# Layer-1 edge pass of a graph network: state sums interleaved with the next block, semaphores for drains, powers in PSUM

## What is computed

```python
# N, E, NIN, H, C = (6250, 100000, 256, 8, 32); per edge, then summed by target node dst
e     = edge_attr @ We                         # E x 256
k, v  = k[src] + e, v[src] + e
logit = (q[dst] * k).sum(channels)             # E x 8
alpha = softmax of logit over the edges of one dst
out   = segment_sum(v * alpha, dst)
```

## Time and profile before

| | |
|---|---|
| time, median of 3 runs | 5678.94 us (5672.48 to 5680.9) |
| span of the profiled execution | 5673.3 us |
| busy in the span | TensorE 50%, VectorE 67%, ScalarE 25%, GpSimd 60% |
| the edge pass | about 3504 to 5156 us of the span |
| in it, per 100 us | VectorE 90.2, TensorE 82.2, GpSimd 77.1, ScalarE 24.1 us busy; DMA engines 1.01 of the time |

### The profile page before, as it was taken

The page is one execution under the profiler, slowest core; times in us unless marked ns, Lnnn a source line. Parts: engine busy times, 40 slices in busy tenths (PEclk is TensorE's granted clock), DMA queues, the critical chain, the costliest instruction groups (busy, mean ns, idle before and its releaser), DMA issues. The chain is left out here.

```text
span 5673.3 us, 49658 instructions
## 1 busy us (share of the span) xinstructions
PE 2860.0 (50%) x13052; PEld 2232.1 (39%) x13052; DVE 3824.3 (67%) x6117; ACT 1441.9 (25%) x2526; POOL 3388.4 (60%) x3382
## 2 busy tenths in 40 slices
PE   7513200000000000015899986888888888884777
PEld 5412200000000000014677633777776777673456
DVE  7357778786454545546543464989899998995763
ACT  1113333332233333311222211222222222221320
POOL 0267777777777777753440276777777777773200
PEclk9655555555555555556799998999999999896888
DMA  3133344432363333323232355999999999993114
GB/s 101 36 84 108 107 130 148 130 104 83 103 220 110 109 110 109 110 87 124 93 124 68 107 191 191 317 319 323 319 319 321 319 323 318 323 318 113 67 47 148
DMA packets 290231, 961.79 MB, mean 170 GB/s; under 512 B 79248, under 2 KB 119831, under 8 KB 248468
## 3 DMA queue, kind: packets, MB, share of 16 engines
q0 software_dynamic: 171296, 483.60, 28.6%
q1 hardware_dynamic: 118788, 476.59, 24.9%
HBM read 626.03 MB, written 345.69 MB: 171 GB/s over the span
## 5 line engine op out<-in xcount | busy, mean ns | idle before, releaser
L1249 PE MATMUL e_psE<-e_we,e_eaT 128*128 128x256 f32 x3136 | 903.5, 415 | 279.3 <-DVE e_wv L1148 179.3
L1111 POOL DMA_INDIRECT e_kv<-kv,rec x784 | 875.7, 1117 | 266.3 <-issue 253.7
L779 POOL DMA_INDIRECT g_g<-t,rec x784 | 777.1, 991 | 254.0 <-issue 253.7
L779 POOL DMA_INDIRECT g_g<-t,dst_of x784 | 743.6, 949 | 259.3 <-issue 257.2
L1249 PEld LDWEIGHTS e_psE<-e_we,e_eaT 128*128 128x128 f32 x3136 | 649.4, 210 | 400.7 <-ACT e_eaT L1192 299.4
L1407 PE MATMUL j_psM<-ident,tail 128*128 128x128 f32 x32 | 7.2, 416 | 1149.0 <-PEq L53 1149.0
L1250 PE MATMUL e_psE<-e_kv,ident 128*128 128x256 f32 x1568 | 509.8, 409 | 0.0
L816 DVE TENSOR_TENSOR_SCAN g_wv<-g_fx,g_wv 128x2176 f32<-128x2176 f32 x98 | 459.0, 4684 | 0.2 <-issue 0.2
L1407 PEld LDWEIGHTS j_psM<-ident,tail 128*128 128x128 f32 x32 | 6.8, 322 | 1149.8 <-issue 1149.8
L1118 POOL DMA_INDIRECT e_q<-q,q_of x392 | 370.9, 946 | 119.7 <-issue 119.7
L956 ACT ACTIVATE g_st<-g_wv 128x2048 f32<-128x2048 f32 x98 | 375.9, 3836 | 0.0
(11 more groups left out here) (519 smaller groups left out, 6620.8 us busy)
## 6 DMA issues: line engine op xcount, KB each, us to landing
state<-e_st SPq DMA_DIRECT2D x98, 1088.0 KB, 6.2
e_ea<-in_edge_attr SPq DMA_DIRECT2D x98, 896.0 KB, 9.8
state_f<-g_st SPq DMA_DIRECT2D x49, 1088.0 KB, 4.4
state_b<-g_st SPq DMA_DIRECT2D x49, 1088.0 KB, 4.3
m_work<-xs SPq DMA_DIRECT2D x119, 128.0 KB, 2.3
ys<-m_work SPq DMA_DIRECT2D x119, 128.0 KB, 1.7
xs<-g_ta SPq DMA_DIRECT2D x28, 512.0 KB
g_g<-t,rec POOLq DMA_INDIRECT x784
```

What stands on the lines that cost most here:

```text
L779: pool.indirect_dma_start(g[:, u, j, :], None, tab, bass.IndirectOffsetOnAxis(ap=at_, axis=0)).then_inc(gat[u], 16)
L1111: pool.indirect_dma_start(kv[:, u, b, :], None, c.kv, bass.IndirectOffsetOnAxis(ap=c.rec[:, t, 1:2], axis=0)).then_inc(gkv[u][b // 4], 16)
L1249: nc.tensor.matmul(half, eaT[:, m, j, k, :], we[:, k, :], start=(k == 0), stop=False)
```

## The change

It concerns `edge_pass` alone; the arithmetic stays the same.

- VectorE: the chain of L1176 of a block (`chain`) and its denominators' scan (`denominators`) are issued between the instructions of the next block, one `step` at a time. Drains are replaced by semaphores that VectorE raises and waits for itself (`chained`, `weighed`, `multiplied`, `logits`, `scanned`, `carried`, `entered`). The reduction is split in two halves; the second addition of values moves behind `ex`. `wv` gets two buffers.
- ScalarE makes the exponential twice: into `cw` as before, and for the products into `pw`, which lies in a PSUM bank. Maximum and denominator of a block are stored after the next block's start.
- TensorE has three transpose banks instead of four (the fourth is `pw`), `eaT` has two buffers, and block n+1 is transposed between the two halves of block n.
- GpSimd gathers the first four keys and values, then the queries, then the other four, with a wait before each.
- SyncE loads the attributes three blocks ahead instead of two.

The diff; the removed lines of VectorE, ScalarE and TensorE stand above in the kernel, and are left out here.

```diff
--- before.py
+++ after.py
@@ -1037,22 +1037,24 @@
...
-        eaT = sb("eaT", [P, 4, 2, 2, P])
+        eaT = sb("eaT", [P, U, 4, 2, 2, P])
...
-        psT = [pb(f"psT{n}") for n in range(4)]
+        psT = [pb(f"psT{n}") for n in range(3)]
...
+        pw = pb("pw")[:, 0:H * B].rearrange("p (h b) -> p h b", h=H)
...
-        wv, before = sb("wv", [P, B, D]), sb("before", [P, D])
+        wv, before = sb("wv", [P, U, B, D]), sb("before", [P, D])
...
-        ld, gq0, gq1, eg0, eg1, used, exd, cwd, dnd, std, so0, so1, free, dump, tp, tcp, ep, ed = (
-            sem(n) for n in ("ld", "gq0", "gq1", "eg0", "eg1", "used", "exd", "cwd", "dnd", "std", "so0",
+        ld, gq0, gq1, eg0, eg1, exd, cwd, dnd, std, so0, so1, free, dump, tp, tcp, ep, ed = (
+            sem(n) for n in ("ld", "gq0", "gq1", "eg0", "eg1", "exd", "cwd", "dnd", "std", "so0",
...
-        q_used = sem("q_used")
...
+        chained, weighed, multiplied, logits, scanned, carried, entered = (sem(n) for n in (
+            "chained", "weighed", "multiplied", "logits", "scanned", "carried", "entered"))
...
@@ -1077,50 +1079,68 @@
...
-            def store(i, u):
-                blk = i * U + u
+            def store(blk, u, older):
...
-                sp.wait_ge(so[1 - u], (i + 1) * 16)
+                sp.wait_ge(so[1 - u], older * 16)
...
+            def ahead(blk, u, older):
+                sp.wait_ge(tp, blk * 4 + 8)
+                c.alone(sp)
+                load_attributes(blk + 3, 1 - u)
+                store(blk, u, older)
...
-            with sp.Fori(0, NBLK // U - 1) as i:
-                for u in range(U):
-                    sp.wait_ge(tp, (i * U + u + 1) * 4)
-                    c.alone(sp)
-                    load_attributes(i * U + u + U, u)
-                    store(i, u)
-            store(NBLK // U - 1, 0)
-            store(NBLK // U - 1, 1)
+            sp.wait_ge(tp, 4)
+            c.alone(sp)
+            load_attributes(2, 0)
+            ahead(0, 0, 1)
+            with sp.Fori(0, NBLK // U - 2) as i:
+                ahead(i * U + 1, 1, i + 1)
+                ahead(i * U + 2, 0, i + 2)
+            store(NBLK - 3, 1, NBLK // U - 1)
+            store(NBLK - 2, 0, NBLK // U)
+            store(NBLK - 1, 1, NBLK // U)
...
+            def keys_and_values(blk, half):
+                for b in range(4 * half, 4 * half + 4):
+                    t = blk * B + b
+                    pool.indirect_dma_start(kv[:, blk % U, b, :], None, c.kv, bass.IndirectOffsetOnAxis(
+                        ap=c.rec[:, t, 1:2], axis=0)).then_inc(gkv[blk % U][half], 16)
...
-                u = blk % U
...
-                    pool.wait_ge(used, blk - U + 1)
+                    pool.wait_ge(ed, 4 * (blk - U) + 6)
...
-                for b in range(B):
-                    t = blk * B + b
-                    pool.indirect_dma_start(kv[:, u, b, :], None, c.kv, bass.IndirectOffsetOnAxis(
-                        ap=c.rec[:, t, 1:2], axis=0)).then_inc(gkv[u][b // 4], 16)
+                keys_and_values(blk, 0)
...
-                    pool.wait_ge(q_used, blk - U + 1)
+                    pool.wait_ge(logits, 3 * (blk - U + 1))
...
-                    pool.indirect_dma_start(q[:, u, m, :], None, pairs, bass.IndirectOffsetOnAxis(
-                        ap=c.q_of[:, t // 2:t // 2 + 1], axis=0)).then_inc(gq[u], 16)
+                    pool.indirect_dma_start(q[:, blk % U, m, :], None, pairs, bass.IndirectOffsetOnAxis(
+                        ap=c.q_of[:, t // 2:t // 2 + 1], axis=0)).then_inc(gq[blk % U], 16)
+                if blk >= U:
+                    pool.wait_ge(ed, 4 * (blk - U) + 8)
+                    c.alone(pool)
+                keys_and_values(blk, 1)
...
+            flat = lambda a: a.rearrange("p h b -> p (h b)")
+            back = lambda a: a.rearrange("p h b -> p (h b)")[:, ::-1]
...
@@ -1132,64 +1152,121 @@
...
+            def chain(n, u, b):
+                if b == 0:
+                    v.wait_ge(free, n + 1)
+                    v.wait_ge(weighed, n + 1)
+                else:
+                    v.wait_ge(chained, n * (B - 1) + b)
+                nc.vector.scalar_tensor_tensor(
+                    out=st[:, u, b, 0:D], in0=st[:, u, b - 1, 0:D] if b else before[:], scalar=kept[:, u, b:b + 1],
+                    in1=wv[:, u, b, :], op0=ALU.mult, op1=ALU.add).then_inc(std if b == B - 1 else chained, 1)
+            def denominators(n, u):
+                v.wait_ge(entered, n + 1)
+                v.wait_ge(act_mt, n)
+                nc.vector.tensor_tensor_scan(flat(den[:]), flat(kept_h[:, u]), flat(cw[:]), 0.0, ALU.mult,
+                                             ALU.add).then_inc(dnd, 1)
+            def one_block(n, u, gathered, later):
+                def step(b):
+                    if later:
+                        chain(n - 1, 1 - u, b)
+                def half_of(half):
+                    quad = psE[:, half * 1024:(half + 1) * 1024]
+                    return quad, q[:, u, 2 * half:2 * half + 2, :].rearrange("p m n -> p (m n)")
+                def with_queries(half):
+                    quad, q4 = half_of(half)
+                    v.wait_ge(ep, n * 4 + 2 * half + 2)
+                    tt(q4, quad, q4, ALU.mult).then_inc(multiplied, 1)
+                def values(half):
+                    quad, _ = half_of(half)
+                    tt(wv[:, u, 4 * half:4 * half + 4, :], kv[:, u, 4 * half:4 * half + 4, D:2 * D],
+                       quad.rearrange("p (j n) -> p j n", j=4), ALU.add).then_inc(ed, 2)
+                def sum_channels(half):
+                    _, q4 = half_of(half)
+                    v.wait_ge(multiplied, 2 * n + half + 1)
+                    nc.vector.tensor_reduce(at[:, :, 1 + 4 * half:5 + 4 * half].rearrange("p h b -> p b h"),
+                                            q4.rearrange("p (j h k) -> p j h k", j=4, k=C), AX.X, ALU.add).then_inc(logits, 1)
+                step(0)
+                if later:
+                    denominators(n - 1, 1 - u)
+                    v.wait_ge(exd, n)
+                    v.wait_ge(scanned, 2 * n)
+                copy(at[:, :, 0], mt[:, :, B]).then_inc(logits, 1)
+                v.wait_ge(gq[u], gathered)
+                with_queries(0)
+                step(1)
+                values(0)
+                step(2)
+                with_queries(1)
+                step(3)
+                sum_channels(0)
+                step(4)
+                sum_channels(1)
+                step(5)
+                v.wait_ge(marked, n + 1)
+                v.wait_ge(logits, 3 * n + 3)
+                nc.vector.tensor_tensor_scan(flat(mt[:]), flat(parted[:, u]), flat(at[:]), 0.0, ALU.add,
+                                             ALU.max).then_inc(scanned, 1)
+                step(6)
+                if later:
+                    v.wait_ge(act_mt, n)
+                v.wait_ge(scanned, 2 * n + 1)
+                nc.vector.tensor_tensor_scan(back(top[:]), back(parted_next[:, u]), back(mt[:]), 0.0, ALU.add,
+                                             ALU.max).then_inc(scanned, 1)
+                step(7)
+                v.wait_ge(scanned, 2 * n + 2)
+                tt(ex[:], at[:], top[:], ALU.subtract).then_inc(exd, 1)
+                values(1)
+                by_head = lambda a: a.rearrange("p (h k) -> p h k", k=C)
+                v.wait_ge(cwd, 2 * n + 1)
+                if later:
+                    v.wait_ge(std, n)
+                tt(by_head(before[:]), by_head(st[:, 1 - u, B - 1, 0:D]), cw[:, :, 0].unsqueeze(2).to_broadcast([P, H, C]),
+                   ALU.mult).then_inc(carried, 1)
+                v.wait_ge(cwd, 2 * n + 2)
+                v.wait_ge(ed, 4 * n + 8)
+                products = wv[:, u].rearrange("p b (h k) -> p b h k", k=C)
+                tt(products, products, pw.rearrange("p h b -> p b h").unsqueeze(3).to_broadcast([P, B, H, C]),
+                   ALU.mult).then_inc(weighed, 1)
+                v.wait_ge(carried, n + 1)
+                if later:
+                    v.wait_ge(dnd, n)
+                tt(cw[:, :, 0], cw[:, :, 0], den[:, :, B], ALU.mult).then_inc(entered, 1)
+            one_block(0, 0, nrows, False)
+            with v.Fori(0, NBLK // U - 1) as i:
+                one_block(i * U + 1, 1, (i + 1) * nrows, True)
+                one_block(i * U + 2, 0, (i + 2) * nrows, True)
+            one_block(NBLK - 1, 1, NBLK // U * nrows, True)
+            chain(NBLK - 1, 1, 0)
+            denominators(NBLK - 1, 1)
+            for b in range(1, B):
+                chain(NBLK - 1, 1, b)
+            v.wait_ge(std, NBLK)
+            v.wait_ge(act_mt, NBLK)
...
+            def transposed_attributes(blk, u):
...
+                    nc.scalar.activation(eaT[:, u, m, :, :, :].rearrange("p a b c -> p (a b c)"), psT[m % 3][:, :],
...
@@ -1200,62 +1277,86 @@
...
+            def powers(n):
+                act.wait_ge(exd, n + 1)
...
```

(88 more changed lines are left out.)

61 lines of the change are left out of this document (removed).

## The result

The changed kernel takes **5596.97 us** (median of 4 runs, 5589.97 to 5600.22), the kernel before 5679.28 us in the same runs: ratio 0.9853, interval 0.9841 to 0.9865. The gain is 82 us, not the 30 us forecast.

The account below looks back on a forecast made before the run. VectorE was taken to bound the kernel before (16.57 us a block), transfers the changed one (16.3): 98 x (16.57 - 16.3) = 26; 5673.3 - 26 - 4 at the pass's end, plus 5.6 outside the span: 5649 us, range 5562 to 5684.

Parts of the forecast that it names:

- VectorE 13.8 us: Layer 1's edge pass: VectorE's work per block after the change, 13.8 us, with bounds 13.4 and 16.2.
- Waits and queues: Edge pass: TensorE's transposes, SyncE's earlier loads and GpSimd's third wait stay hidden; missed cover for powers costs about 0.5 us.
- GpSimd 15.3 us (14.96 to 15.9): Edge pass: GpSimd's need per block, twelve gathers at 14.96 us plus 0.3 us of remaining holds.
- rival 2: Edge pass: gathers start into scattered chain sums; decides from 0.13 us per gather; at 0.2 us, 5757 us; chance 0.11.
- The transfers' floor of 16.3 us: Edge pass: transfers need 16.3 us a block (16.1 to 16.5) and become the bound, VectorE waiting for gathers.
- The end of the pass, 4 us: From the last gather's issue to the last state's end: 24.7 us instead of 28.6, so 4 us less.
- Rival 1: Edge pass: transfers give way and GpSimd becomes the bound, 5551 us, or 5609 with GpSimd at 15.9; chance 0.19.
- Rival 4: Edge pass: the chain waits for itself, VectorE stays at 16.2 us a block, 5640 to 5660 us; chance 0.05.
- rival 3: Edge pass: transfers have no room, the period stays at 16.5 to 16.6 us, 5670 to 5679 us; chance 0.10.

Follow-up runs that it names:

- experiment 7: Changed kernel with half of the attributes loaded and two of the four query gathers a block left out: 5393.71 us (0.9497).
- experiment 6: Changed kernel, order kept, with 14 drains a block put back behind VectorE's products, reductions, second additions and chain sums: 5741.46 us (1.011).
- experiment 4: Kernel before with powers in PSUM and seven of eight chain instructions left out: 5566.3 us; the same with half of the attributes loaded: 5522.4 us.
- light_chain: Kernel before with powers in PSUM and seven of the eight chain instructions of a block left out: 5566.3 us (0.9807).
- experiment 1: Changed kernel with powers back in SBUF: 5821.12 us (1.0244); kernel before with only the powers moved to PSUM: 5680.19 us (1.0003).
- experiment 2: Changed kernel with the four query gathers of a block replaced by plain SyncE loads of the same size: 5767.15 us (1.0145).

## Why the prediction was wrong, point by point

- *VectorE 13.8 us.* Right: 13.53 in a block without holes, 13.49 as the bound (experiment 7). The overlap of 0.08 us, read from two instructions of before, carried over to all. The rule of the Trainium skill weighed there (page "VectorE: DVE Perf Modes", section "The DRAIN you can't avoid"), by which the time is the plain sum of durations, is not borne out: by it experiment 7 would have stayed at about 15.5 us. The same section adds that a next operation that isn't held starts earlier, which the prediction left out and which is what these rows show. An explicit drain does cost it, and more (experiment 6).
- *Waits and queues.* Right in the main: the transposes between the halves, the loads three blocks ahead and the third wait of GpSimd show hardly any cost (in 3700 to 4900 TensorE waits 21.5 us for attributes to land, where nobody was to wait; GpSimd's waits come to 0.14 us a block); the powers never hold up VectorE (L1242 has 0.0 us of idle time before it).
- *GpSimd 15.3 us (14.96 to 15.9).* Right in kind, 0.36 us too low: 15.66. The 2.3 us gather is gone as said. What is left is 8 x 0.054 + 4 x 0.018 = 0.50 us of holds instead of 0.3, 0.14 us of waits for a buffer, and 0.06 because the gap is 0.305 and not 0.30. Three quarters of the 0.50 are what rival 2 named, gathers that begin in one of the chain's instructions with two SBUF inputs, most of the rest those that begin in L1237; it is 0.04 us a gather, and the decision lay at 0.13. This term did not decide the forecast, but with the transfers' floor right the sum would have gone by its 15.3 us and given 5551, 46 us too fast.
- ***The transfers' floor of 16.3 us: this step failed.*** It is 15.5 us (experiment 4), below GpSimd's 15.66, and it is what made 30 us out of 82: the prediction let VectorE, once freed, wait for transfers at 16.3 us, and what bounds the changed kernel is GpSimd at 15.66, with the transfers just below. The reasoning had three parts. The burst of 285 GB/s was taken as a ceiling, and with it the 11 us that it lasts; but 3700 to 4900 in light_chain has the same order of transfers and passes 7% more. The gathers' backlog in the burst was taken as proof that nothing more could pass; but a backlog after the burst only says that the gathers were late by the burst. And spare capacity was counted as the time in which the rate fell to GpSimd's own, with the rate of the burst itself held fixed; it rose. Single microseconds of after, about three and four behind the issue of a store (4226.29):

```profile
4229.00:4230.00 1.00, 1.00 (x7) 0.87 (x6) 1.00 (x2) 0.15 (x1) 0.80 (x1) 1.00 1.09 437
4230.00:4231.00 1.00, 1.00 (x6) 0.90 (x5) 0.98 (x5) 0.18 (x2) 0.89 (x1) 1.00 0.99 417
```

  Averaged over the blocks from 4000 to 4600 by the time since the store's issue, the first seven microseconds pass 382 to 435 GB/s in after and 311 to 390 before; the slow part behind it has 235 to 327 in after and 181 to 271 before. So the whole burst is faster, and not its tail alone; in light_chain, with the order of before, the first seven microseconds have 373 to 436 GB/s. Why more of the same packets pass in the burst as soon as VectorE is lighter stays open; a queue of gathers that is never empty is one guess, and no run isolates it.
- *The end of the pass, 4 us.* 3.3 us, from the last gather to the last store 25.2 us where 24.7 were summed.
- *The rivals.* Rival 1 is what happened, with GpSimd between its two values (15.3 and 15.9), and the transfers giving way to within 0.2 us of it. It had a chance of 0.19. Its "for" was right: 5.32 MB in 15.66 us is 340 GB/s. Its "against", the backlog in the burst, was the misreading above. The Trainium skill's page "DMA: Bandwidth & Descriptors", section "Specifications", with about 358 GB/s from HBM for a core, took this side. Its estimate of 14.9 us a block was too fast against the 15.5 measured; the 338 to 342 GB/s of three kernels stay below its figure, while the gathers alone at 386 GB/s and single microseconds of 417 and 437 stand above it, so it is no limit for short stretches here. With the powers in SBUF (experiment 1) the kernel was slower than rival 2's 5757 (5821 us), though for the most part by the product L1242 and not by the chain. Rival 4 is excluded by the spacing of 0.40 us, rival 3 by the period.

What would it have taken? A view of before that I had not put into the sum: all waits for a landing from 3700 to 4900, and all of VectorE for TensorE.

```profile
PEld e_psT L1239 <- DMA e_ea<-ea_tail: 1.4, 2, 0.7
PE e_psT L1239 <- DMA e_ea<-ea_tail: 0.6, 2, 0.3
DVE e_q L1147 <- PE e_psE L1250: 0.3, 2, 0.2
```

In 72 blocks nothing waited for keys and values or for queries to land, and VectorE waited 0.3 us for TensorE. In after the same stretch has 134.1 us of waits for `e_kv` and 150.0 for `e_psE`. A floor of the transfers 0.3 us under the period, in blocks that differ among themselves (some had windows of idle engines, others none), should have shown up in some of those 72; that is an argument, and experiment 4 is the proof. I used the absence of holes to find the bound, and not to judge the distance to the next one.

## To carry to other kernels

A DMA share of 1.0 and a backlog behind a burst do not measure the capacity of the transfers as long as another engine sets the pace: before a floor is put into a sum, ask whether that engine ever waits for a landing, or make its work lighter and see what rate then passes. An operand in PSUM instead of SBUF took VectorE out of the way of GpSimd's gathers; it was worth 1.2 us of GpSimd's time a block in the old order and 2.4 in the new one, where the gather happened to begin ahead of the product. Semaphores on VectorE in place of drains were worth 0.26 us for each on the mean. When two resources come out within a per cent of each other, a relief of one can measure zero (here that of the transfers did), and both have to be lifted in one experiment to see what lies under them.

## What the runs showed of the hardware

- The DMA share is 1.01 at 321 GB/s, 1.02 at 340 and 342, 1.03 at 338, and 1.01 at 306 (experiment 2): it does not tell how near the ceiling is. Where it was well below 1 (0.93 at 304, 0.96 at 318), GpSimd was the bound and the transfers had room.
- This mixture of gathers of 2 KB rows, 1088 KB stores and 1 MB loads has a ceiling of 338 to 342 GB/s on the mean, reached in three kernels, one of them in the order of before; the landing takes longer there (the stores' median is 8.2 us in after, 6.2 before).
- A gather that starts under a VectorE instruction with both tensors in SBUF is held until that instruction is over: 2.32 us instead of 0.95 under L1166. From L1237 the hold passed on to L1242 (3.31 us); from L1166 to L1168, and from L1242 to L1247, it did not, though no drain stands between those either.
- With one of the two tensors in PSUM the gather isn't held: 0.94 us under L1242 in the changed kernel.
- An explicit drain between two VectorE instructions costs 0.26 us behind one of 1024 elements; behind one of 256 it costs from 0.18 us up. Fourteen of them cost 3.6 us a block.
